# Second attention of a four-layer block: the remainder written in two pieces with a wait each, and a 1 MB weight load issued in four

## What is computed

```python
def _L1_xattn_ref(latents, context, Wq, Wk, Wv, Wo):      # H, KV, HD = 16, 4, 96
    hidden = jnp.concatenate([context, latents], axis=1)   # 768 keys
    ...
    scores = jnp.einsum('bkgqd,bksd->bkgqs', q, k) * scale
    attn = jax.nn.softmax(scores.astype(jnp.float32), axis=-1).astype(q.dtype)
    out = jnp.einsum('bkgqs,bksd->bkgqd', attn, v)
    ...
    return out @ Wo.T
def _L2_xattn_ref(query, key, value, Wq, Wk, Wv, Wo):
    q = (query @ Wq).reshape(b, sq, NUM_HEADS, HEAD_DIM).transpose(0, 2, 1, 3)
```

## Time and profile before

| | |
|---|---|
| three executions | 1303.97, 1296.91, 1304.06 us |
| median | 1303.97 us |
| the profiled execution | 1296.22 us |
| its span, first to last instruction | 1294.5 us |
| mean granted TensorE clock over the span | 0.98 of full speed |
| share of the span in which the engines were busy | TensorE 92%, DVE 70%, ACT 49%, POOL 40% |
| second attention, first scores to last output product | about 622.6 to 923 us |

### The profile page before, as it was taken

The page is one execution under the profiler, slowest core; times in us unless marked ns, Lnnn a source line. Parts: engine busy times, 40 slices in busy tenths (PEclk is TensorE's granted clock), DMA queues, the critical chain, the costliest instruction groups (busy, mean ns, idle before and its releaser), DMA issues.

```text
span 1294.5 us, 19370 instructions
## 1 busy us (share of the span) xinstructions
PE 1197.0 (92%) x7154; PEld 936.9 (72%) x7154; DVE 909.0 (70%) x1682; ACT 637.1 (49%) x1046; POOL 516.1 (40%) x385
## 2 busy tenths in 40 slices
PE   6999999989999989989989889997899999999986
PEld 5878788868888777777868779786775444777733
DVE  6688789866798899864577856885456774543287
ACT  3556556634566455631454534564235778323252
POOL 5136364725245457444151714232635000355212
PEclk9999999999999989999999989998998999999999
DMA  5578779945689577840376936877212000482000
GB/s 187 114 153 168 145 158 171 201 90 114 135 156 187 115 151 144 161 118 21 91 164 115 200 76 116 149 133 149 61 69 75 1 1 2 129 195 74 1 1 33
DMA packets 356188, 146.38 MB, mean 113 GB/s; under 512 B 327744, under 2 KB 334048, under 8 KB 356096
## 3 DMA queue, kind: packets, MB, share of 16 engines
q1 hardware_dynamic: 356096, 145.15, 53.6%
HBM read 57.17 MB, written 5.37 MB: 48 GB/s over the span
## 4 chain that ended last, share of the span: by engine, by line
PE 37%; DVE 7%; ACT 2%; issue 2%; POOL 1%; DMA 1%; SPq 0%; DVEq 0%; ACTq 0%; POOLq 0%
PE ps L863 5%; PE ps L1993 5%; PE ps L1559 3%; PE ps L1585 3%; PE ps L891 3%; PE ps L832 3%; PE ps L2006 2%; DVE p L1146 2%; DVE rows_and_turned L1133 2%; PE ps L2291 1%; PE ps L1541 1%; PE ps L817 1%; PE ps L808 1%; PE ps L1570 1%; PE ps L1493 1%
## 5 line engine op out<-in xcount | busy, mean ns | idle before, releaser
L863 PE MATMUL ps<-kT,qT 128*128 128x512 f32 (+3 forms) x1152 | 240.6, 344 | 40.8 <-DVE p L1146 38.3
L863 PEld LDWEIGHTS ps<-kT,qT 128*128 128x128 f32 (+1 forms) x1152 | 201.0, 191 | 97.0 <-DVE p L1146 43.5
L987 ACT ACTIVATE ps<-ps,rows_and_turned 128x768 f32<-128x768 f32 x192 | 168.0, 875 | 193.7 <-DVE rows_and_turned L1133 193.7
L995 ACT ACTIVATE p<-ps,rows_and_turned 128x768 f16<-128x768 f32 x192 | 172.9, 900 | 166.8 <-ACT ps L987 101.3
L1133 DVE TENSOR_REDUCE rows_and_turned<-ps 128x1 f32<-128x768 f32 x192 | 183.3, 955 | 96.4 <-PE ps L863 96.4
L891 PE MATMUL ps<-pT,vv 128*128 128x256 f16 (+1 forms) x1728 | 225.7, 277 | 10.4 <-DMA pT<-p 7.0
L1146 DVE SCALAR_TENSOR_TENSOR p<-ps,rows_and_turned,p 128x768 f16<-128x768 f32 x192 | 193.5, 1008 | 7.0 <-ACT p L995 7.0
L891 PEld LDWEIGHTS ps<-pT,vv 128*128 128x128 f16 (+1 forms) x1728 | 169.8, 108 | 31.7 <-issue 14.0
L726 POOL TENSOR_TENSOR wo<-raw,one 128x512 fp32r<-128x512 f32 (+1 forms) x48 | 50.2, 1047 | 252.7 <-PE ps L832 222.0
L817 PE MATMUL ps<-xT,wq 128*128 128x512 f32 x528 | 144.0, 408 | 0.0
L832 PE MATMUL ps<-wo,oT 128*128 128x512 f32 (+1 forms) x396 | 114.9, 416 | 3.1 <-DVE x L1035 3.1
(11 more groups left out here) (276 smaller groups left out, 1933.8 us busy)
## 6 DMA issues: line engine op xcount, KB each, us to landing
raw<-in_l_wq SPq DMA_DIRECT2D x44, 256.0 KB, 3.4
f2raw<-in_f_w SPq DMA_DIRECT2D x11, 776.0 KB, 4.7
rows_and_turned<-in_m_w SPq DMA_DIRECT2D x11, 768.0 KB, 5.5
raw<-in_l_wo SPq DMA_DIRECT2D x32, 256.0 KB, 3.3
pT<-p SPq DMA_TRANSPOSE x192, 3.7
raw<-in_l_wo SPq DMA_DIRECT2D x16, 192.0 KB, 3.3
w3gu<-rows_and_turned SPq DMA_DIRECT2D x11, 256.0 KB, 2.8
ctxraw<-in_ctxT SPq DMA_DIRECT2D x2, 1024.0 KB, 7.7
```

The lines of the kernel that those rows point to most:

```text
L863: last = nc.tensor.matmul(sc[:, lo:hi], query(A, h, qp)[:, r * P:(r + 1) * P], keys(A, h // A.g)[0:hd, kp, b, lo:hi], start=(qp, kp) == PA ...
L987: nc.scalar.activation(score_banks(n), score_banks(n), ACT.Exp, bias=nmax[:, n % 32:n % 32 + 1], accum_out=rsum[:, n % 32:n % 32 + 1]).the ...
L995: nc.scalar.activation(p16[:, n % 3, HI], score_banks(n), ACT.Copy, scale=rden[:, n % 32:n % 32 + 1]).then_inc(sem("att_half"), 1)
```

## The change

It has two parts, both for the second attention and what is issued in it.

1. The remainder of a step is written by two instructions, columns 0 to 511 and columns 512 to 767. Each counts `low` up by one, so the count of A1 doubles. `scores(n)` waits for the first piece of n - 2 ahead of its first three matmuls, and for the second piece ahead of the other three. The transpose waits for both pieces. The first attention is as before.
2. The load of the third attention's query weights is four DMAs of 256 KB. At the place of the old load a list of four is filled; each of the next four steps (58 to 61) issues one, behind the transpose of the step. POOL waits for all four.

```diff
+        if before:
+            count["low"] *= 2
...
+        def low_done(A, m, pieces):
+
+            return 2 * m + pieces if A is A1 else m + 1
...
                 if A is A1 and entry == ("o", 14, 0):
                     sp.wait_ge(sem("w3_done"), 4 * A1.stored)
-                    att2_early_sp(sp, l2wq_raw, "l2_wq")
+                    pieces.extend(range(KT))
...
-                att_wait(sp, A, "low", m + 1)
+                att_wait(sp, A, "low", low_done(A, m, 2))
...
+            pieces = []
             for n in range(-1, A.items + 1):
                 if 1 <= n:
                     turn(n - 1)
+                if pieces:
+                    att2_early_sp(sp, l2wq_raw, "l2_wq", pieces.pop(0))
                 for j, entry in A.load_at.get(n, []):
                     load(j, entry)
...
                 if n >= 2:
-                    wait("low", n - 1)
+                    wait("low", low_done(A, n - 2, 1))
                 sc = ps[:, 2 * (n % 2):2 * (n % 2) + 2, :].rearrange("p a c -> p (a c)")
                 for lo, hi in ((0, 512), (512, S)):
+                    if n >= 2 and lo and A is A1:
+                        wait("low", low_done(A, n - 2, 2))
...
-                nc.vector.scalar_tensor_tensor(p16[:, m % 3, LO], score_banks(m), rden[:, m % 32:m % 32 + 1],
-                                               p16[:, m % 3, HI], ALU.mult, ALU.subtract).then_inc(sem("att_low"), 1)
+                for lo, hi in ((0, 512), (512, S)) if A is A1 else ((0, S),):
+                    nc.vector.scalar_tensor_tensor(p16[:, m % 3, LO, lo:hi], score_banks(m)[:, lo:hi],
+                                                   rden[:, m % 32:m % 32 + 1], p16[:, m % 3, HI, lo:hi], ALU.mult,
+                                                   ALU.subtract).then_inc(sem("att_low"), 1)
...
-        def att2_early_sp(sp, to, name):
-
-            sp.dma_start(to[:], t[name].rearrange("(k p) n -> p k n", p=P)).then_inc(sem(name), 16)
+        def att2_early_sp(sp, to, name, k=None):
+
+            given = t[name].rearrange("(k p) n -> p k n", p=P)
+            if k is None:
+                sp.dma_start(to[:], given).then_inc(sem(name), 16)
+            else:
+                sp.dma_start(to[:, k], given[:, k]).then_inc(sem(name), 16)
 
         def att2_split_hi_pool(g, w, given, name):
-            g.wait_ge(sem(name), 16)
+            g.wait_ge(sem(name), 16 * KT if name == "l2_wq" else 16)
```

## The result

| | before | changed |
|---|---|---|
| median of 5 executions | 1303.05 us (1296.91 to 1304.06) | 1290.98 us (1287.57 to 1292.26) |
| ratio | | 0.9909, 95% interval 0.9882 to 0.9937 |
| profiled execution, its span | 1296.22, 1294.5 us | 1290.98, 1289.3 us |

The change takes 12 us off, 0.6 to 1.2%. The forecast was a median of 1293, in 1285 to 1301, from a gain of 8.4 us. The mean granted clock is 0.984.

The account below looks back on a forecast made before the run. TensorE bounds it, idling in job-less steps' 3.27 us rings and at a late transpose near 884 to 901. Part 1's 2.4 plus part 2's 6.0 is 8.4 off 1296.2: 1287.8; between two levels, 1293 was named, range 1285 to 1301.

Parts of the forecast that it names:

- two levels: Executions of the kernel before were taken to lie near 1296 or 1304 us, untouched by the change.
- Same: The outcome that the measurement, which tells about 1%, shows no change from before; chance 0.70.
- Ring and pieces: Second attention: remainder pieces of 0.74 and 0.48 us, the pair 1.14, job-less score-maximum-remainder cycle 3.0 in place of 3.27.
- The nine plain rings: Job-less steps (scores 6 to 10, 25, 26, 41, 42), each 0.27 us shorter, 2.4 us in all.
- The other steps of part 1: Three waits behind DVE-filled steps gain 0.3 us; two remainders in the DVE chain at 746 cost 0.3.
- I take the full clock: After the value product once at 895.29, the next comes in 3.4 us instead of 6.06: 2.7 less.
- The 0.6 that the pieces were to give back: The four load pieces delay transposes 58 to 61, returning 0 to 0.8 us; 0.6 taken.
- Pieces crowd the transposes: Rival: the 4.9 us stall spreads over transposes 58 to 61; part 2 gives 2.5, total 4.9; chance 0.17.
- DVE becomes the bound: Rival: the split costs 0.25 us a step, part 1 gives 0, only part 2's 6 remains; chance 0.13.
- A wait inside the group: Rival: the wait among six matmuls exposes weight loads, 0.19 us in 45 steps; 1.8 slower overall; chance 0.08.
- More goes than that, since another fall of the clock also stays away: Rival: another fall of the granted clock is avoided too, 12 us less, 1292 or 1284; chance 0.07.
- The signs: Listed checks: pieces 0.74 and 0.48, rings 3.0, projection steps 3.43, ACT's wait at most 1 us, clock 1.00 near 893.

Follow-up runs that it names:

- e4: The kernel before, run again unchanged as a candidate for a second trace; 1301.3 us, ratio 1.0.
- e13: The changed kernel run once more for a second trace; 1289.56 us, ratio 0.9903.
- e10: The kernel before, with the three 48-column VectorE instructions one step later in the second attention; 1294.24 us against 1304.64, ratio 0.9922.
- e11: The changed kernel, with the three 48-column VectorE instructions one step later in the second attention; 1285.33 us, ratio 0.9867.
- e7: The changed kernel, with the remainder in two pieces in the first attention too; 1290.45 us, ratio 0.9923.
- e5: The changed kernel, with the 1 MB query-weight load in one DMA issued after the loop; 1291.71 us against 1300.27, ratio 0.9922.
- e1: The changed kernel with the load in one DMA at its old place, so only the remainder split; 1294.72 us against 1300.84, ratio 0.9952.
- e3: As e1, but the scores wait for both pieces ahead of all six matmuls; 1305.32 us, ratio 1.0035.
- e2: The changed kernel with the remainder in one instruction, so only the load in four; 1294.09 us against 1300.84, ratio 0.9953.
- e8: The kernel before, with eight unread matmuls filling TensorE's idle time in each of nine steps without a job; 1298.89 us, ratio 0.999.
- e12: The changed kernel, with last expert-weight store later, first attention's remainder split, and three 48-column instructions moved one step later; 1280.44 us against 1304.64, ratio 0.9824.
- e6: The changed kernel, with the last store of rounded expert weights one step later; 1289.3 us, ratio 0.9911.

## Why the prediction was right, and where it was off

**The time** lay in the range and 2 us from the value named, and part of that is luck. The sum had 8.4 us and 12 were measured. The value named, 1293, stood between two levels that do not exist; 8.4 off the measured median of before, 1303.05, would have been 1294.7. Within the sum one term was missing and one too large. "Same" had 0.70; the measured ratio is 0.9909, and its interval lies on both sides of 1% less.

**Ring and pieces: right.** Pieces of 0.742 and 0.474 against 0.74 and 0.48, the pair 1.13 to 1.14 against 1.14, the ring 3.01 to 3.03 against 3.0. The nine plain rings gave 2.42 (16.53 to 15.15 us in steps 6 to 10, and 1.04 in 25, 26, 41, 42), forecast 2.4. The rings at 57 to 60 gave 1.1 and lost it again behind the transpose of 56, as said.

**The other steps of part 1: sizes off.** Forecast were 0.3 more and 0.3 less. Measured: four more rings (13, 20, 45, 52) gave 1.1; seven full steps of DVE (16, 18, 19, 32, 34, 35, 36) cost 0.13 each, 0.9; steps 28 to 30 cost 0.7. That is 0.5 back, where I had nothing.

**Missing from the sum: the 48-column instructions.** Steps 12 and 44 gave 1.4 us more (4.71 and 4.62 to 3.96 and 3.95) in the two traces that were compared; the sum had nothing for it. Against other executions of before it is more: from step 43 to 46, 14.1 us in e4 and 10.3 in the changed kernel. With it, part 1 gave 3.2 from step 5 to 56 by the traces (forecast 2.4) and 6.1 by the times. I read the trace of before as typical, and it was a good one: 1296.22 where the median is near 1303, with one instruction hit at each place and no fall of the clock there. By the ratios of e13, e10 and e11, two fifths of the change's gain go with this collision (an estimate: 0.97% with it, 0.55% without, each 0.25 to 0.3 either way).

**Part 2: mechanism right, 6.0 was 4.6.** The landing is 3.8 and ACT's wait is gone. The step that failed is "I take the full clock". Counted from the issue of the transpose of 56 (885.96 here, 884.70 before), the scores of 61 start after 5.8 us, where the forecast had 5.7. But the clock fell at 892.3, in the middle of them. From their start to the value product it took 1.61 in place of 1.0, so that product comes 3.2 earlier (forecast 3.9). From there to the next value product it took 4.59, where 6.06 was to become 3.4. The idle stretch ahead did not shrink to almost none: the one ahead of the value product went, and the one ahead of the scores of 61 grew from 1.43 to 2.34, since the shorter rings of 57 to 60 reach it sooner and the transpose of 56 stayed where it was. In e7, where the clock stayed up behind the same stretch, the two distances are 1.15 and 3.41 and steps 56 to 63 take 6.3 less than before. So the sum holds where the full clock is granted, and whether it is differs between executions. The 0.6 that the pieces were to give back did not come.

**The two levels: wrong.** Four executions looked like two levels; 34 show a spread. Part of what spreads them is what the change touches: how many of the small instructions are hit, and the clock behind. The forecast took the spread as untouched by the change.

**The rivals.** Pieces crowd the transposes: refuted. Those of 58 to 60 land in 3.8 to 4.6. That of 61 takes 5.7, over the 5.5 named as a sign of being wrong, but it takes 6.0 in e5 without any piece. That a DMA's 2.0 us hold the queue did not come either: a piece held SP's queue for 0.81 to 0.99. (The section cited for it is on DMAs issued from GpSimd; these are issued from SP.) DVE becomes the bound: refuted for the whole, e1 alone gives 6.1; it is true of seven steps. A wait inside the group: refuted by e1 beside e3. "More goes than that, since another fall of the clock also stays away" (0.07) came closest in its number: 12 less was measured. Near 842 its mechanism is at work too, though not in the profiled execution of before: of the traces with the old start of the scores, e2, e3, e4 and e8 have that fall.

**The signs.** The lengths of the pieces, the rings, the full steps and ACT's wait came as listed. The granted clock of 1.00 near 893 did not.

**What stays open.** The first attention differs by 6 us between executions of the same code. It has 24 such small instructions, of which 8 to 11 lasted over 0.9 us in each of the 14 traces; moving them was not tried. That the shorter rings bring POOL and DVE apart at step 44, and less surely at 12, is read from positions in the traces (hit in one of six against five of five); why is not derived. What decides whether the clock falls behind an idle stretch of 1.5 to 2.3 us is not shown either. The gain of e12 beyond the 17 us or so in the second attention (265.9 against a mean of 282.9) is not placed.

## What to carry to other kernels

Where a consumer waits for a producer that writes in one instruction, split the instruction at the consumer's own order and let it start on the first part; price it as the start it brings forward, times the steps where that wait is the ring, less the longer end times the steps where the producer is full. Take a big load away from ahead of the transfer that the compute waits for; one late load did as well here as four small ones. And before a small difference is put down to an edit, look in a second trace of the same kernel for the steps that vary: here a collision of two other engines went with some two fifths of the change's gain, and removing it by itself, a one-step move, gave 0.78%.

## What the hardware showed that I had not expected

- Short DVE instructions (48 columns, 0.19 us) lasted 0.9 to 1.3 us when a GpSimd tensor_tensor had just started, up to 3.46 in the first attention, and never more than 0.19 when none ran. The tensor reductions, the remainders and the exponentials beside the same roundings kept their lengths (0.94, 1.01, 0.88). One longer instruction did not: the scaling of the weights at line 1073 (128x768, both inputs in SBUF) takes 0.95 alone. At 847.7 in the trace of before it started 0.27 after a rounding of POOL had begun, took 1.83 and ended 0.81 behind the rounding's end; in the changed kernel's, at 849.3, it took 1.54. All 14 traces have this in step 49, which takes 4.16 to 4.50, and no run here moved it.
- At step 44 an idle TensorE of 1.96 to 2.15 us was followed by a granted clock of 0.50 (1.2 GHz) for 3.4 us, four times out of four, and one of 0.79 (before) or 0.69 (e6) was not. One of 1.70 at step 6 was followed by a fall in e4 and e2 and by none in before and e10. Ahead of the scores of 61, 2.21 to 2.34 brought a fall in five traces of six, and 1.48 brought one in e2. So the length of the idle stretch did not decide it alone. Rings with 0.99 of idle time each brought no fall at 818 to 833 in any trace, and filling them changed nothing.
- Two DVE instructions in a row overlap by 0.08 us even when they are halves of one, so that the split costs 0.13 a step and not a whole fixed part.
- A wait between matmuls of one group that is met in time does not show in the spacing of full steps (3.38 to 3.44 with, 3.40 to 3.44 without).
